# Embedding a token language-model tower in two halves of the tokens, the second mixed inside the next stage

## The reference, cut to what matters

```python
# 16 x 256 = 4096 tokens, 24 chromosomes ("blocks"), 128 centers each, rows of 128 numbers
pos = position + chromosome * 2.0
w = exp(-(pos[..., None] - centers) ** 2 / (2.0 * exp(log_variances)))   # 3072 centers
w_top, idx = top_k(w, 10); w_top = w_top / sum(w_top)
h = einsum('bnk,bnkd->bnd', w_top, embeddings[idx])                       # the embedding
h = h + attention(layernorm(h))        # latent q and kv, rope, 8 heads, 2 kv heads, causal, 256 keys
h = h + experts(layernorm(h))          # 64 experts, 42 kept by the router, exact gelu
```

## Time and profile before

| | |
|---|---|
| median of 3 runs | 1898.24 us (1894.03 to 1899.62) |
| the profiled execution's own time | 1896.82 us |
| its span, first to last instruction | 1894.9 us |
| busy in the span: PE, DVE, ACT, POOL | 94%, 83%, 81%, 74% |
| mean granted TensorE clock | 0.967 |

### The profile page before, as it was taken

The page is one execution under the profiler, slowest core; times in us unless marked ns, Lnnn a source line. Parts: engine busy times, 40 slices in busy tenths (PEclk is TensorE's granted clock), DMA queues, the critical chain, the costliest instruction groups (busy, mean ns, idle before and its releaser), DMA issues.

```text
span 1894.9 us, 29977 instructions
## 1 busy us (share of the span) xinstructions
PE 1781.7 (94%) x8423; PEld 1427.7 (75%) x8423; DVE 1569.8 (83%) x2194; ACT 1528.9 (81%) x2733; POOL 1410.9 (74%) x837
## 2 busy tenths in 40 slices
PE   6468699987999999999999999999999999999998
PEld 4345467765788888888888888888888888888886
DVE  8559788876688888888888888888888888888888
ACT  2158688887888888888888888888888888888886
POOL 4343176654389888898888888688888888888886
PEclk9968799996899999999999999999999999999999
DMA  7510000002533333333333333333333333333332
GB/s 222 155 29 18 1 1 0 0 4 51 134 112 130 120 114 118 135 114 114 139 111 116 134 111 121 125 115 112 136 111 116 133 111 124 125 111 127 122 111 67
DMA packets 107017, 191.88 MB, mean 101 GB/s; under 512 B 13750, under 2 KB 86438, under 8 KB 90790
## 3 DMA queue, kind: packets, MB, share of 16 engines
q1 hardware_dynamic: 104894, 186.77, 29.4%
q0 software_dynamic: 2048, 4.20, 0.8%
HBM read 179.40 MB, written 11.53 MB: 101 GB/s over the span
## 4 chain that ended last, share of the span: by engine, by line
PE 77%; DVE 6%; ACT 3%; issue 2%; POOL 2%; POOLq 0%; DVEq 0%; ACTq 0%
PE f_ps_h L2263 12%; PE f_ps_h L2265 12%; PE f_ps_h L2264 12%; PE f_ps_y L2276 12%; PE f_ps_y L2277 12%; PE f_ps_y L2278 12%; PE ps_s L1486 2%; DVE neg_max L1372 2%; PE ps_p L1439 2%; PE ps_ko L1472 1%; POOL y_sum L2117 1%; PE ps_qy L1447 1%; PE ps_qy L1429 1%; DVE g_lo L2217 1%; DVE q_t L1341 1%
## 5 line engine op out<-in xcount | busy, mean ns | idle before, releaser
L2117 POOL TENSOR_TENSOR y_sum<-y_sum,weighed 128x512 f32<-128x512 f32 x504 | 1028.2, 2051 | 102.1 <-DVE weighed L2209 95.0
L2217 DVE TENSOR_TENSOR g_lo<-gelu_out,g_hi 128x1024 fp32r<-128x1024 f32 x512 | 815.7, 1593 | 86.1 <-ACT g_hi L2158 70.1
L2149 ACT ACTIVATE gelu_out<-f_ps_h,b_t 128x512 f32<-128x512 f32 x1024 | 648.6, 685 | 194.5 <-PE f_ps_h L2265 192.2
L2158 ACT ACTIVATE g_hi<-gelu_out 128x1024 fp32r<-128x1024 f32 x512 | 541.9, 1059 | 0.0
L2209 DVE SCALAR_TENSOR_TENSOR weighed<-f_ps_y,b_t,c_row 128x512 f32<-128x512 f32 x504 | 375.4, 745 | 120.3 <-PE f_ps_y L2278 119.1
L2276 PE MATMUL f_ps_y<-g_hi,w_hi 128*128 128x512 f32 x1024 | 400.1, 391 | 3.2 <-DVE g_lo L2217 2.6
L2263 PE MATMUL f_ps_h<-x_hi,w_hi 128*128 128x512 f32 x1024 | 399.8, 390 | 2.6 <-ACT e L1689 2.6
L2264 PE MATMUL f_ps_h<-x_lo,w_hi 128*128 128x512 f32 x1024 | 399.4, 390 | 0.0
L2265 PE MATMUL f_ps_h<-x_hi,w_lo 128*128 128x512 f32 x1024 | 399.3, 390 | 0.0
L2277 PE MATMUL f_ps_y<-g_lo,w_hi 128*128 128x512 f32 x1024 | 398.5, 389 | 0.0
L2278 PE MATMUL f_ps_y<-g_hi,w_lo 128*128 128x512 f32 x1024 | 398.4, 389 | 0.0
(11 more groups left out here) (228 smaller groups left out, 1608.0 us busy)
## 6 DMA issues: line engine op xcount, KB each, us to landing
c_row<-comb_rows SPq DMA_DIRECT2D x124, 1024.0 KB, 4.8
w_raw<-in_w SPq DMA_DIRECT2D x256, 128.0 KB, 4.4
c_row<-comb_rows SPq DMA_DIRECT2D x16, 256.0 KB, 5.7
by_slot<-b_zeros SPq DMA_DIRECT2D x1, 3072.0 KB, 13.2
b_gauss_s<-by_slot SPq DMA_DIRECT2D x12, 256.0 KB, 5.4
mixed_rows<-mixed SPq DMA_DIRECT2D x12, 256.0 KB, 2.2
out<-h SPq DMA_DIRECT2D x8, 256.0 KB, 4.2
cent<-in_centers SPq DMA_DIRECT2D x1, 1536.0 KB, 7.0
```

Source lines behind the costliest of these rows:

```text
L2117: pool.tensor_tensor(y_sum[:, w, g, :], y_sum[:, w, g, :], weighed[:, r % 2, :], ALU.add).then_inc(added, 1)
L2149: last = act.activation(gelu_out[:, r % GELUS, c, :], ps_h[:, r % 2, c, :], ACT.Gelu, bias=b_t[:, c, bass.ds(e, 1)])
L2158: act.activation(g_hi[:, r % RING], gelu_out[:, r % GELUS], ACT.Copy).then_inc(hi_ready, 1)
L2217: dve.tensor_tensor(g_lo[:, r % RING], gelu_out[:, r % GELUS], g_hi[:, r % RING].bitcast(F32), ALU.subtract).then_inc(lo_ready, 1)
```

## The change

The tokens are taken in two halves of 16 tiles. `SLOTS` becomes 128 for a block and a half, so the slots are 3072 for each half and 6144 as before. Each half has a semaphore of its own for its scatters, and rows of its own in DRAM (`early_rows`, `late_rows`, as `mixed_rows[0]` and `[1]`).

In `embed_by_block` SP now loads the first half's six groups after its 16 scatters. PE turns and mixes them, and ACT makes both copies. The turned tiles and the products have one PSUM bank each, where they had two each. The product with `doubts` stands behind these mixes. `edges` moves to the front of DVE's program, and slots are computed for each half. SP also clears a spare part of `late_rows` (1 MB).

In `front` SP loads the second half's six groups (`late_s`); PE turns and mixes them after it has folded the matrices, ACT makes both copies ahead of its first `root_x`, and SP stores them. POOL fetches rows of the first 16 tiles after the first half's stores, of the others after all stores. `table` is placed where it outlives the stage.

```diff
-SLOTS = 256
+HALVES = 2
+SLOTS = 128
...
             for t in range(TILES):
                 pool.wait_ge(chosen, t + 1)
                 pool.indirect_dma_start(by_slot, bass.IndirectOffsetOnAxis(ap=dest[:, t:t + 1], axis=0),
-                                        gauss[:, t, :], None).then_inc(scattered, 16)
+                                        gauss[:, t, :], None).then_inc(scattered[t // HALF_TILES], 16)
...
+            sp.dma_start(mixed_rows[1][HALF_SLOTS:, :].rearrange("(t p) d -> p t d", p=P),
+                         zeros[:].unsqueeze(1).broadcast_to([P, HALF_TILES, P])).then_inc(spare_cleared, 16)
+            sp.wait_ge(scattered[0], 16 * HALF_TILES)
+            load_slots(sp, by_slot, 0, gauss_s, slots_in)
+            for i in range(LOADS_OF_HALF):
                 sp.wait_ge(mixed_copied, i + 1)
+                store_mixed(sp, mixed, mixed_rows[0], i, stored)
...
+            for k in range(HALVES):
+                half = slice(k * HALF_TILES, (k + 1) * HALF_TILES)
+                last = dve.scalar_tensor_tensor(out=slot[:, half], in0=slot[:, half], scalar=k * HALF_SLOTS - 1.0,
+                                                in1=spill[:, half], op0=ALU.add, op1=ALU.subtract)
...
+            def turn(i):
+                pe.wait_ge(slots_in[i], 16)
+                after(pe, copied, i)
...
+            def mix(i):
+                pe.wait_ge(copied, i + 1)
+                after(pe, mixed_copied, i)
...
+        @block.sync
+        def _(sp):
+            sp.wait_ge(scattered[1], 16 * HALF_TILES)
+            load_slots(sp, by_slot, 1, late_s, late_in)
+            for i in range(LOADS_OF_HALF):
+                sp.wait_ge(late_copied, i + 1)
+                store_mixed(sp, mixed, mixed_rows[1], i, stored)
...
             act.activation(warm[:], wsum[:, 0:1], ACT.Sqrt)
+            copy_late_turned(0)
+            for i in range(LOADS_OF_HALF):
+                if i + 1 < LOADS_OF_HALF:
+                    copy_late_turned(i + 1)
+                copy_late_mixed(i)
             root_x(0)
...
+            def turn_late(i):
+                pe.wait_ge(late_in[i], 16)
+                after(pe, late_t_copied, i - 1)
...
+            def mix_late(i):
+                pe.wait_ge(late_t_copied, i + 1)
+                after(pe, late_copied, i - 1)
...
+            turn_late(0)
+            for i in range(LOADS_OF_HALF):
+                if i + 1 < LOADS_OF_HALF:
+                    turn_late(i + 1)
+                mix_late(i)
             turn_x(0)
```

More of the change, by code:

```diff
@@ L443, in _, with copy_turned @@
                 exponentials(q)
-            for i in range(LOADS):
+            def copy_turned(i):
                 act.wait_ge(turned, i + 1)
@@ L505, in _ @@
             dve.tensor_copy(dest[:], slot[:])
-            dve.tensor_scalar(source[:], slot[:], float(SPILL - 1), None, ALU.min).then_inc(dest_ready, 1)
+            for k in range(HALVES):
+                half = slice(k * HALF_TILES, (k + 1) * HALF_TILES)
+                last = dve.tensor_scalar(source[:, half], slot[:, half], float(-k * HALF_SLOTS), float(HALF_SLOTS - 1),
+                                         ALU.add, ALU.min)
+            last.then_inc(dest_ready, 1)
             for q in range(QUADS):
@@ L589, in _ @@
             gather(0)
-            pe.wait_ge(counted, 1)
-            pe.matmul(ps_b[:, 0:BLOCKS], earlier[:], counts[:], start=True, stop=True).then_inc(based, 1)
-            for q in range(1, QUADS):
-                gather(q)
             pe.wait_ge(edges_ready, 1)
@@ L596, in _ @@
                       stop=True).then_inc(edges_spread, 1)
+            pe.wait_ge(counted, 1)
+            pe.matmul(ps_b[:, bases_at], earlier[:], counts[:], start=True, stop=True).then_inc(based, 1)
+            for q in range(1, QUADS):
+                gather(q)
+            def turn(i):
+                pe.wait_ge(slots_in[i], 16)
+                after(pe, copied, i)
+                for s in range(QUAD):
+                    last = pe.transpose(ps_turned[:, s * P:(s + 1) * P], gauss_s[:, i * QUAD + s, :], ident[:])
+                last.then_inc(turned, 1)
+            def mix(i):
+                pe.wait_ge(copied, i + 1)
+                after(pe, mixed_copied, i)
+                for s in range(QUAD):
+                    last = pe.matmul(ps_mixed[:, s * DIM:(s + 1) * DIM], gauss_t[:, i % 2, s * P:(s + 1) * P],
+                                     table[:, i * QUAD + s, :], start=True, stop=True)
+                last.then_inc(mixed_ready, 1)
+            pe.wait_ge(table_in, 16)
+            turn(0)
+            for i in range(LOADS_OF_HALF):
+                if i + 1 < LOADS_OF_HALF:
+                    turn(i + 1)
+                mix(i)
             pe.wait_ge(doubts_ready, 1)
@@ L712, in body @@
             def body(pool):
-                pool.iota(source[:], pattern=[[P, TILES]], base=0, channel_multiplier=1)
+                for k, first in ((0, 0), (1, HALF_SLOTS)):
+                    pool.iota(source[:, k * HALF_TILES:(k + 1) * HALF_TILES], pattern=[[P, HALF_TILES]], base=first,
+                              channel_multiplier=1)
                 pool.wait_ge(prec, 1)
```

174 lines of the change are left out of this document (101 added, 73 removed).

## The result

The changed kernel took 1880.85 us (median of 4 runs, 1879.3 to 1881.7) and the one before 1898.02 (4 runs, 1894.03 to 1899.62) in the same sitting: a ratio of 0.9915, 95% interval 0.9898 to 0.9931, 17.2 us. The forecast was 1881.0 with 1874 to 1889. The profiled execution took 1881.43, its span 1879.7 us at a mean granted clock of 0.970. The span before was 1894.9, so the two spans differ by 15.2 us, and 13.9 of them are already there at the first root of x: 106.39 before, 92.46 now.

What follows compares the result with a forecast made beforehand. The bound was taken as one chain from POOL's scatters through loads, mixes and barriers to the first root. Root 16.3 us earlier plus 1 us of clock takes 1896.82 to 1879.5; the median, 1.4 higher, 1881, range 1874 to 1889.

Steps and rivals of the forecast that it cites:

- Start of DVE's program: Ahead of the selection: edge instructions and half-wise slots delay the first scatter by 0.95 us, bounds 0.7 to 1.3.
- The first half costs nothing: In `embed_by_block`: first-half mixes end near 64.5 us, covered by DVE's selection and doubts, with the flag ready at 67.5.
- the first half outlasts the doubts: Rival in `embed_by_block`: slow clock or loads queued behind the new 1 MB cost 2.5 to 5 us; 12%.
- Barriers: Between flag and `front`: register load, both barriers and branches take 6.35 us, so `front` starts at 73.9.
- what would make the forecast wrong: Signs: scatter gaps over 0.3 us, doubts' product waiting for mixes, longer barriers with a late flag, ACT pacing the fill.
- Second half in `front`: Folding takes 4.2 us and hides the load; six groups take 11.2 us at 1.33 us steady period; root at 90.1.
- the slower rival: In `front`: loads come one by one at 5.4 us each, root at 108.7 or 141, up to 1933 us; 3%.
- Sum to the root: First root of x moves from 106.39 to 90.1 us, 16.3 us earlier.
- Clock: First quad behind the root: PE's shorter idle gap gains at most 4 us from a higher clock; 1 us counted.
- The rule on shared queues: At 46 to 58 us: transfers sharing 16 engines could hold scatters up by 13.3 us; by the trace nearly nothing.

Runs made afterwards that it cites:

- f1: Changed kernel without the two wide broadcast loads of centres and precisions (3 MB): 1880.65 us on chip 2, 0.9920 of the kernel before.
- f3: Changed kernel with attention weights loaded by 14 transfers rather than 28, same bytes: 1880.83 us on chip 2, 0.9919 of the kernel before.
- g1: Changed kernel with wide loads moved to the general path, clearing behind the first half's loads, ACT's first copy before its last exponentials: 1879.85 us, 0.9901 of the kernel before.
- f4: Changed kernel with the second half also loaded, turned, mixed and stored in the embedding's block: 1891.55 us on chip 2, 0.9979 of the kernel before.
- f2: Changed kernel with 16 more loads of 512 bytes on SP: 1884.83 us on chip 2, 0.9937 of the kernel before.

## Why the prediction was right, step by step

*Start of DVE's program*, 0.95 us: the first scatter came at 24.81 against 24.01, so 0.80, within the bounds of 0.7 and 1.3.

*The first half costs nothing*: this failed by 2.0 us, the flag being ready at 69.48 and not at 67.5. The step put the loads at 46.6 and forgot that ACT's copies stand behind its exponentials, which the order of the code shows. By its numbers the first copy was due at 50.7 and came at 55.13, 4.5 us late; the last mix was due at 64.5 and ended at 69.11, 4.6 us late. So the pace between them was as forecast, PE's long times for the first groups included. The loads were 3.2 us late by the queues, as f1 shows, but the copies held the first half anyway, as f1, f3 and g1 show together. It was the rival "the first half outlasts the doubts", a little under its 2.5 to 5 us, and for neither of its reasons: the step had allowed for the slow start, and the late loads did not count.

*Barriers*, 6.35 us: 8.13 were measured. The row from which it came has a flag that was known 23 us before the last mix ended, so that POOL's `DRAIN` of 2.68 us, which follows its reading of the flag, was over by then. Where the flag comes last, this `DRAIN` is on the path; f4 gives the hidden case again (6.04), and the other traces the open one (7.8 to 8.25). I had named it among what would make the forecast wrong, but gave it no price. Together `front` began at 77.61 and not at 73.9.

*Second half in `front`*: from the start of `front` to the first late turn 4.03 us (4.2 forecast), from there to the end of the last mix 10.3 (81.64 to 91.93; 11.2 forecast), in which the steady period of 1.33 was exact and PE's short times began earlier. No wait for the loads: the slower rival (loads one by one) is out, since their issue took 4.68 us in all. No wait for statistics: they were ready at 88.67. That is 11.1 us behind the start of `front` and not 8.6, for DVE waited for the gathers until 87.19; beside the loads they are slower (f4, with no loads there, has its root after 8.5 us), and 3.8 us of slack hid it.

*Sum to the root*: 16.3 forecast, 13.9 measured. The 2.4 us are 2.0 for the flag and 1.8 for the barriers, less 1.1 in the fill and 0.3 between the last mix and the root.

*Clock*, 1 us: behind the root lie 1788.5 us before and 1787.2 after, 1.3 less. But the same stretch was 1787.4 to 1790.3 in the six traces of chip 2, so that this 1.3 is not to be told from nothing. The granted clock did fall, to 0.59 in 96 to 100, behind the gap before the first turn of x, and the first products of x took the long times of 1.2 GHz.

*The rule on shared queues.* The row first: in 46 to 58 us, with the share up from 0.17 to 0.84, POOL spent 9.22 us issuing against 9.26 and the last scatter ended at 66.55, so the up to 13.3 us did not come. What did come is that the scatters of the first half landed 3 us later beside the broadcasts: SP's loads, which wait for them, went out 4.6 us behind the 16th scatter, and 1.3 us behind it in f1, which has no broadcasts. Transfers of SP and of GpSimd run on the same 16 engines and interleave (the Trainium skill, "DMA: Bandwidth & Descriptors", section "Issuing engines are not separate DMA queues"). This trace agrees, with those 3 us; they cost nothing, for ACT's copies came later still. The forecast had read from POOL's issue times that scatters are not held up, but those times do not show when a scatter lands.

So on the first chip the mechanism was right: the loads, mixes and stores of 12 groups no longer lie between scatters and barrier, and f4 shows what each half is worth. Its terms were off by 2.0 and 1.8 us one way and 1.4 the other. The median met the forecast to 0.15 us also because it is 17.2 below that of before, where the two profiled executions are 15.4 us apart (1896.82 and 1881.43); part of that closeness is chance.

On chip 5 the forecast of a gain was wrong. There `front` started at 91.22, and the root came 23.1 us later than on the first chip. The forecast took every hand-over between engines at its price in one trace. The change took away the 8 us that DVE had to spare, and put hand-overs of ACT and PE on the path in the stretch in which that chip has its stalls.

## What to carry to other kernels

When an engine takes over a share of another stage's work, look at what stands ahead of it in its own instruction order, not only at whether the engine is idle: in f1 ACT was idle for 4.16 us with a turned tile ready and could not copy it. A barrier costs what its last arrival makes it cost; taking work from in front of it can uncover a step that had been free, here POOL's 2.68 us at the end of its block. That an engine issues its transfers at the old pace does not show that they land at the old pace. Slack on an engine that is off the path can be what absorbs a bad stretch, and a change that uses it up is exposed. And a gain made from fine overlap in the first hundred microseconds should be measured on more than one chip before it is believed: the same program was 0.9909 of its predecessor on one and 1.0024 on another.

## What was not expected of the hardware

Two chips of one kind ran the same program in 1880.91 and 1905.24 us, each repeatably (5 runs within 1.4 us, 10 within 4.7), while the kernel before had 1895 to 1898 there and 1901.7 here. All of it lay between 28 and 110 us, together with some 1,100 missing semaphore updates of 14,300. The long waits are waits for an update that is recorded late: three engines, DVE itself among them, waited for one that came 3.0 us behind the end of its instruction, and ACT for one that came 6.0 us behind. Whether the recording held up the engines, or whether one slow thing there both delays and loses the updates, stays open, and so does whether the program would stall there when nobody records it. The transfers of instructions are not the likely cause: none falls within ACT's 7.25 us, and POOL and SP went on issuing through the stall at 50 us. What would settle it, f1, f2 and f3 on chip 5, is not there, since the later sittings fell on chip 2.
